# Second row half of attention-times-V with the key tiles outer and the channel tiles inner

## The reference

```
q = einsum('bcn,dc->bnd', x1, Wq) + bq
k = einsum('bcn,dc->bdn', x2, Wk) + bk
v = einsum('bcn,dc->bdn', x2, Wv) + bv
attn = softmax(einsum('bnd,bdm->bnm', q, k), axis=2)
out = einsum('bcm,bnm->bcn', v, attn) + x1
```

## Time and profile before

| | |
|---|---|
| median of three runs | 688.51 us (687.49 to 689.01) |
| profiled execution, span from first to last instruction | 687.4 us |
| PE busy | 656.8 us, 96% of the span |
| DVE busy | 475.1 us, 69% |
| ACT busy | 280.7 us, 41% |
| POOL busy | 139.3 us, 20% |
| DMA, share of 16 engines' time | 51.1%, 146 GB/s |
| granted TensorE clock, mean | 0.995 |

### The profile page before, as it was taken

How to read it: one execution, slowest core, us unless ns; L and a number is a source line. 1 busy time by engine, 2 the same in 40 slices (tenths; PEclk the granted TensorE clock), 3 DMA queues, 4 the chain that set the end, 5 groups by cost and what they waited for, 6 DMA issues and landing times.

```text
span 687.4 us, 8392 instructions
## 1 busy us (share of the span) xinstructions
PE 656.8 (96%) x2848; PEld 534.1 (78%) x2848; DVE 475.1 (69%) x503; ACT 280.7 (41%) x367; POOL 139.3 (20%) x58
## 2 busy tenths in 40 slices
PE   5999889999999989999899998999989999899997
PEld 3877668887788868888688886888868888788886
DVE  4889558695686765876758866679567695686641
ACT  5564422355235352354423633337232364234220
POOL 0302210063001440032400433005130063101200
PEclk9999989999999999999999999999999999999999
DMA  8400932749328482285624675255941749326351
GB/s 317 187 1 12 265 108 61 193 137 243 102 86 232 116 234 91 84 237 124 197 92 123 197 170 190 75 139 158 229 153 61 174 142 248 107 80 149 73 179 56
DMA packets 94874, 100.04 MB, mean 146 GB/s; under 512 B 8336, under 2 KB 69776, under 8 KB 94864
## 3 DMA queue, kind: packets, MB, share of 16 engines
q1 hardware_dynamic: 94864, 99.91, 51.1%
HBM read 51.64 MB, written 16.78 MB: 100 GB/s over the span
## 4 chain that ended last, share of the span: by engine, by line
PE 81%; DVE 6%; issue 4%; SPq 3%; ACT 3%; DMA 2%; DVEq 0%; ACTq 0%
PE acc_ps L731 39%; PE acc_ps L700 25%; PE s_ps L670 8%; PE s_ps L678 4%; PE s_ps L679 4%; DVE pt_lo L455 4%; SPq L208 3%; DMA stage<-in_ctx_dram 2%; ACT pt_hi L302 2%; ACT xs_hi L302 1%; DVE probs L497 1%; DVE blocks L506 1%; PE s_ps L794 1%; DVE negmax L490 1%; ACT probs L337 0%
## 5 line engine op out<-in xcount | busy, mean ns | idle before, releaser
L731 PE MATMUL acc_ps<-pt_hi,vt_hi 128*128 128x512 f32 x512 | 202.0, 395 | 17.5 <-DVE pt_lo L455 17.5
L731 PE MATMUL acc_ps<-pt_hi,vt_lo 128*128 128x512 f32 x512 | 200.5, 392 | 0.0
L731 PE MATMUL acc_ps<-pt_lo,vt_hi 128*128 128x512 f32 x512 | 200.4, 391 | 0.0
L731 PEld LDWEIGHTS acc_ps<-pt_hi,vt_hi 128*128 128x128 f32 x512 | 96.6, 189 | 44.0 <-DVE pt_lo L455 24.1
L337 ACT ACTIVATE probs<-s_ps,negmax 128x1024 f32<-128x1024 f32 x64 | 71.4, 1116 | 128.4 <-DVE negmax L490 128.4
L271 POOL TENSOR_TENSOR xs_lo<-stage,xs_hi 128x1024 fp32r<-128x1024 f32 x35 | 91.1, 2612 | 156.0 <-ACT xs_hi L302 156.0
L731 PEld LDWEIGHTS acc_ps<-pt_hi,vt_lo 128*128 128x128 f32 x512 | 96.7, 189 | 20.4
L731 PEld LDWEIGHTS acc_ps<-pt_lo,vt_hi 128*128 128x128 f32 x512 | 96.8, 189 | 19.8
L271 POOL TENSOR_TENSOR pt_lo<-pt_raw,pt_hi 128x1024 fp32r<-128x1024 f32 x14 | 41.0, 2946 | 327.5 <-ACT pt_hi L302 327.5
L700 PE MATMUL acc_ps<-wv_hi,xs_hi 128*128 128x512 f32 x256 | 99.9, 390 | 0.0
L700 PE MATMUL acc_ps<-wv_hi,xs_lo 128*128 128x512 f32 x256 | 99.7, 389 | 0.0
(11 more groups left out here) (49 smaller groups left out, 602.4 us busy)
## 6 DMA issues: line engine op xcount, KB each, us to landing
pt_raw<-blocks SPq DMA_DIRECT2D x240, 128.0 KB, 2.4
stage<-in_ctx_dram SPq DMA_DIRECT2D x32, 512.0 KB, 5.3
o_sb<-in_x_dram SPq DMA_DIRECT2D x64, 256.0 KB, 3.3
out_dram<-o_sb SPq DMA_DIRECT2D x64, 256.0 KB, 2.6
stage<-in_x_dram SPq DMA_DIRECT2D x28, 512.0 KB, 5.9
blocks<-in_x_dram SPq DMA_DIRECT2D x4, 512.0 KB, 8.6
pt_raw<-in_L_xattn_Wv_dram SPq DMA_DIRECT2D x4, 256.0 KB, 8.0
pt_raw<-in_L_xattn_Wk_dram SPq DMA_DIRECT2D x1, 128.0 KB, 3.4
```

Source lines behind the costliest of these rows:

```text
L731: mm = nc.tensor.matmul(acc_ps[:, c % BANKS, :], v[:, m, cols], p[:, m, :], start=(m == 0 and v is vt_hi and p is pt_hi), stop=(m == MT - ...
```

## The change

The second row half runs with m outside and c inside: `out_row(b, 1, m)` gives the parts of all four channel tiles for one key tile, 12 matmuls. `k_next` stands before row 2, the four scores behind rows 4 to 7. The number and kind of matmuls stay as they are. The first half (h = 0) and the q projection are not touched, nor are ACT, POOL and SP.

On DVE `out(b, 0, 3)` moves up between the low parts of pairs 1 and 2, the low part of x2's last tile moves ahead of the low part of pair 3, and the four `out(b, 1, c)`, which stood apart, stand together behind `turn(nb, 1)`.

```
@@ dve batch @@
                 out(b, 0, 2)
-                for j in range(PAIRS - 1):
-                    p_lo(b, 1, j)
-                p_lo(b, 1, PAIRS - 1)
+                p_lo(b, 1, 0)
+                p_lo(b, 1, 1)
+                out(b, 0, 3)
+                p_lo(b, 1, 2)
                 if not last:
                     low_x2(nb, KT - 1).then_inc(s_x2lo_last, 1)
-                out(b, 0, 3)
-
-                out(b, 1, 0)
+                p_lo(b, 1, 3)
                 if not last:
                     dve.wait_ge(s_qlo, nb + 1)
                     k_sum(nb)
                     k_low(nb)
-                out(b, 1, 1)
+                    neg_max(nb, 0)
+                    normalise(nb, 0)
+                    neg_max(nb, 1)
+                    turn(nb, 0)
+                    normalise(nb, 1)
+                    neg_max(nb, 2)
+                    turn(nb, 1)
+                for c in range(CT):
+                    out(b, 1, c)
                 if last:
-                    out(b, 1, 2)
-                    out(b, 1, 3)
                     return
-                neg_max(nb, 0)
-                normalise(nb, 0)
-                neg_max(nb, 1)
-                turn(nb, 0)
-                out(b, 1, 2)
-                normalise(nb, 1)
-                neg_max(nb, 2)
-                turn(nb, 1)
                 normalise(nb, 2)
                 neg_max(nb, 3)
                 turn(nb, 2)
-                out(b, 1, 3)
                 normalise(nb, 3)
                 turn(nb, 3)
@@ pe @@
+            def out_row(b, h, m):
+                for c in range(CT):
+                    out_part(b, h, c, m)
...
-                for c in range(CT):
-                    for m in range(MT):
-                        if not last:
-                            if (c, m) == (1, 0):
-                                k_next(nb)
-                            if (c, m) == (2, 3):
-                                scores_first(nb, 0)
-                            if (c, m) == (2, 6):
-                                scores_first(nb, 1)
-                            if (c, m) == (3, 1):
-                                scores_next(nb, 2)
-                            if (c, m) == (3, 5):
-                                scores_next(nb, 3)
-                        out_part(b, 1, c, m)
+                for m in range(MT):
+                    if m == 2 and not last:
+                        k_next(nb)
+                    out_row(b, 1, m)
+                    if not last:
+                        if m == 4:
+                            scores_first(nb, 0)
+                        elif m == 5:
+                            scores_first(nb, 1)
+                        elif m == 6:
+                            scores_next(nb, 2)
+                        elif m == 7:
+                            scores_next(nb, 3)
```

## The result

The changed kernel takes 716.29 us, the median of four runs (711.02 to 720.15), against 688.32 us of before (four runs, 687.49 to 689.01): a ratio of 1.0405, with a 95% interval from 1.0372 to 1.0439. It is slower by 4%. The forecast was 713 us, with a range from 694 to 728. The profiled execution took 712.89 us with a span of 711.1; in six more executions of the same kernel the median was 716.23.

The account below looks back on a forecast made before the run. PE was taken as the bound, 79.8 of 82.51 us a turn. -8.4 + 27.3 - 2 + 2.5 = +19.4 gave 707.9 us as median, with +5 for clock falls 713 us; range 694 to 728.

Parts of the forecast that it names:

- The waits for the low parts go, 2.7 us a turn: At the start of half 1, PE's waits for DVE's low parts, 2.7 us a turn, go in six turns.
- Bank 3 takes their place, 1.3 us: After nine matmuls of half 1, PE waits for `out(b, 0, 3)` to free bank 3: 1.3 us in all.
- The late x2 load: At half 1, a later x2 load adds to the bank 3 wait; 0.7 us taken.
- `turn(nb, 3)` ends at E + 9.6 and PE waits 3.9 us: After the next batch's first V matmul issues (E), a late residual delays `turn(nb, 3)`; PE waits 3.9 us, +27.3 over seven turns.
- The point of E + 5.7: Latest end of `turn(nb, 3)`, counted from issue of the next batch's first V matmul, at which PE need not wait.
- First batch -2: At half 1 of the first batch, between nothing and 6.7 us is gained; -2 us taken.
- tail +2.5: At the very end, `out(7, 1, 3)` waits for its residual until 2.5 us after PE's end: +2.5 us.
- The clock, two falls, +5: PE's standstill at m = 5 to 7 lowers its clock in two of seven turns, 2.5 us each: +5 us.
- The rival at 725 us: Rival: PE's clock falls in each of the seven turns, giving 725 us; chance 0.18.
- The faster one, hidden slack: Rival: unseen slack from `turn(nb, 3)` to V's last low part leaves PE no wait there: 681 us; chance 0.10.
- The residual hidden: Rival: at the end of half 1 the residual is not waited for, PE waits 1.2 us: 687 us; chance 0.07.
- the matmuls slow down as banks change: Rival: PE's matmuls themselves slow down as banks change every three of them; no size given; chance under 0.02.

Follow-up runs that it names:

- `out(b, 0, 3)` first: Changed kernel with `out(b, 0, 3)` on DVE ahead of the low part of pair 1, not behind it: 712.92 us.
- DVE's order alone: Changed kernel with `out(b, 1, 2)` and `out(b, 1, 3)` moved behind `turn(nb, 3)` and `out(b, 1, 1)` behind `neg_max(nb, 3)` on DVE, SP unchanged: 717.83 us.
- the delay of n = 4: Kernel before with four more DVE instructions (about 4.5 us) between `out(b, 1, 3)` and `normalise(nb, 3)`: 723.21 us, ratio 1.053.
- the first experiment: Changed kernel with SP issuing the residual load of tile 3 of half 1 before the store of tile 0: 688.7 us, ratio to before 1.0007.
- the two delays in the kernel before: Kernel before with one or four more DVE instructions between `out(b, 1, 3)` and `normalise(nb, 3)`: 689.81 us with one, 723.21 us with four.
- with SP's: DVE's order alone, plus SP's `move` of the next half 0 ahead of the stores of tiles 2 and 3: 680.66 us, ratio to before 0.9898.

## Why the prediction was right, step by step

**The waits for the low parts go, 2.7 us a turn: right.** No turn after the first batch has one. In the first batch one is left, as forecast.

**Bank 3 takes their place, 1.3 us: right in kind, a little high.** From the starts of PE's matmuls the wait was 0.58, 0.58, 0.96, 1.70, 0.57 and 0.94 us in the six turns, 0.9 on average: 0.6 wherever nothing else was late, which is the base of the prediction's term. An `out` beside POOL, which no row of before showed, has its row now (DVE, then POOL):

```profile
515.06 2.62 DVE L455 TENSOR_TENSOR pt_lo<-pt_raw,pt_hi 128x1024 fp32r<-128x1024 f32 x1 [0.72 <-ACT pt_hi L302]
517.60 0.74 DVE L523 SCALAR_TENSOR_TENSOR o_sb<-acc_ps,bias_v,o_sb 128x512 f32<-128x512 f32 x1
```

```profile
516.82 3.13 POOL L271 TENSOR_TENSOR xs_lo<-stage,xs_hi 128x1024 fp32r<-128x1024 f32 x1 [0.22 <-ACT xs_hi L302]
```

0.74 us, the lower end, while the low part of a pair takes 2.62. This agrees with the Trainium skill, "SBUF — State Buffer", "Who interferes with whom", by which a DVE instruction contends with a POOL instruction that reads SBUF when it has two inputs in SBUF, and not when it has one. The late x2 load was real but rarer than taken. In the turn with 1.70 us, ACT's timeline has it:

```profile
428.31 1.06 ACT L302 ACTIVATE xs_hi<-stage 128x1024 fp32r<-128x1024 f32 x1 [1.12 <-DMA stage<-in_ctx_dram]
```

In three of the six turns, the two with a fall of the clock among them, nothing of it is seen; in the others it adds 0.4 to 1.1. What makes one load land later than another was not tried.

**`turn(nb, 3)` ends at E + 9.6 and PE waits 3.9 us: right.** The `move` began at E + 9.8 to 10.1 and m = 7 at E + 34.2 to 34.6, so the wait was 4.0 to 4.4, 29.5 us in the seven turns where 27.3 were forecast. Two terms are a little short: the residual is issued at E + 0.13 in every turn, where the prediction had +0.03, and it lands after 3.3 to 3.6 us, where it had 3.3; the shortest are on the forecast and the longest put the `move` at E + 10.1. The point of E + 5.7 is bracketed by the runs: E + 5.5 costs nothing (three kernels; 0.15 us in one turn of one of them), E + 7.1 costs 1.4.

**First batch -2, tail +2.5: right in kind.** E of the first turn came 3.1 us earlier than before (115.32 against 118.47). But not all of it by the way that was forecast. The wait for the first low part (1.3 us) and the one for bank 3 stayed; the low clock, which the prediction kept, did not come in this profile, though PE stood 3 us in one piece:

```profile
88.22 0.50 PE L727 MATMUL acc_ps<-pt_hi,vt_hi 128*128 128x512 f32 x1 [2.85 <-DVE o_sb L523]
```

The granted clock is 1.00 from 80 to 100 us, where before it was at half for 6.8 us. In the second profile of the same kernel PE stood 3.4 us there, and the clock fell for 3.4. So part of the gain in the first batch was luck of this execution. At the tail the last `out` waits 2.85 us for its residual and the end is later by about 3.

**The clock, two falls, +5: right for this profile, low for the median.** In the profiled execution it fell in two turns. One of them, as windows with the columns above:

```profile
146.00:149.00 3.00, 0.97 (x4) 0.49 (x3) 3.00 (x5) 1.51 (x3) 2.29 (x1) 0.94 0.00 0
149.00:152.00 3.00, 2.42 (x6) 1.94 (x7) 2.93 (x5) 2.01 (x4) 1.86 (x1) 0.50 0.00 0
152.00:155.50 3.50, 3.50 (x10) 2.73 (x9) 3.50 (x3) 0.00 (x0) 0.62 (x1) 0.50 0.63 142
```

PE stands for most of three microseconds, and the 6.5 that follow run at 1.2 GHz. From one E to the next that turn took 87.56 us and the other 86.63, the four without a fall 84.8 to 85.8. The sum of the measured terms, -3.1 + 29.5 - 10.9 + 4.7 + 2.9 = 23.1, comes near the measured 711.1 - 687.4 = 23.7. (10.9 is what the waits for low parts took in the six turns, 16.2, less 5.3 for bank 3; 4.7 is what the two turns take beyond 352 matmuls and their waits; the turns without a fall take 0.2 beyond them. 2.9 is what the tail grew by.) The median of all runs lies 3 us above the forecast; the mean clock of all the others is lower (0.974 to 0.986 against 0.991), and in the one other that has a profile it fell in three turns and in the first batch. That the forecast met the profiled execution so closely, two falls in seven turns, is luck: the number of falls changes from execution to execution, and two was a guess from one row. The Trainium skill ("TensorE: Matmul & The Clock Gate", "HAM oscillation — how this bites in real kernels") describes a loop whose wait throttles PE anew in each turn. A fall in each turn came in the profiles of two variants, `out(b, 0, 3)` first and DVE's order alone, and not in the two of the changed kernel. The rival at 725 us was too high for all ten runs, and near for the delay of n = 4.

**The rivals.** The faster one, hidden slack, is refuted by the two delays in the kernel before. The residual hidden, forecast at 687 us, is what the first experiment made of the kernel: 688.7 measured. That the matmuls slow down as banks change is refuted by turns of 80.0 us with 79.8 of matmuls.

## What to carry to other kernels

When work is regrouped so that several results end together, look at what stands behind them on every in-order engine: here 5.4 us came onto one path: 0.7 from the scores that stand later on PE, 2.0 from three `out` more in one place, and 2.7 from a load queued behind one store. Neither the busy shares nor the chain of waits of the kernel before showed this path, as it had 1.4 us to spare. Count that spare time for each path into the loop's next turn before moving anything, and move the DMA issues along with the instructions that feed them: DVE's order alone gained nothing, with SP's it gained 36 us on the changed kernel. A loss in the first try does not speak against the idea: the same matmul order with the queues of DVE and SP put right is 3% faster than the kernel before.

## What the runs showed of the hardware

The clock can fall after standstill that is cut into pieces. Waits of 0.2 to 1.8 us with parts of 0.68 us between them, 4 us in all, were followed by a fall in two of seven turns in one execution of the changed kernel and in three of seven in another, and in all seven in two variants. What decides it was not tested: in the first batch 3.0 us of standstill in one piece, behind another of 1.3, was followed by none.

A fall costs less than half of the time it lasts. The two turns with a fall took 2.8 us more for 6.8 us at half clock and 1.6 us more for 3.4, that is 0.41 and 0.46 us for each us at half clock; in the first of them 0.9 us of the low clock lies in a wait of PE.

And the wait for bank 3 varies from turn to turn in one execution: with one wait of 1.4 us left at V's last low part, the turns of the first experiment took 82.3 to 83.4 us, by the bank 3 wait of 0.6 to 1.9.
